# Cross-attention of a decoder block: row maxima of two heads in one reduction, two banks for transposed scores, shifted projections, one-hop rows of maxima

## The chip, the cores and the metric

The kernel runs on one core of a Trainium2 chip. The metric is the time of one execution on the device in microseconds (us), as a median of runs; lower is better.

## What is computed

A decoder layer on x of shape (8, 256, 512): x + self-attention(norm(x)), then x + cross-attention(norm(x), ctx), then x + gated feed-forward(norm(x)) with weights put through an NF4 quantization. The change is mostly in the cross-attention, which treats a batch's (256, 512) matrix as 256 channels by 512 positions:

```python
q = jnp.einsum('oc,bct->bot', Wq, target) + bq[None, :, None]      # 16 heads of 16 channels
k = jnp.einsum('oc,bcs->bos', Wk, source) + bk[None, :, None]
v = jnp.einsum('oc,bcs->bos', Wv, source) + bv[None, :, None]
dot = jnp.einsum('bhdt,bhds->bhts', q, k) / math.sqrt(HEAD_DIM)
mask = target_mask[:, :, :, None] * source_mask[:, :, None, :]
dot = mask * dot - (1.0 - mask) * NEG
amap = jax.nn.softmax(dot, axis=-1) * mask
out = jnp.einsum('bhts,bhds->bhdt', amap, v)
```

So there are 8 batches x 16 heads of 512 x 512 scores.

## The kernel before, in words

The program has three stages behind one another: `self_attention` (until about 1460 us), `cross_attention` (1304 to 1757) and `feed_forward`. Engines run their own instruction lists and wait on semaphores; each list is written out by hand.

In the cross-attention, Q and K of a batch lie in SBUF as stacks: of each head 16 high, 16 high and 16 low rows, then rows for biases and masks, two heads in the two halves of the partitions (even heads at 0, odd ones at 64), so that matmuls of an even and an odd head run beside one another. Row 53 of the Q stack holds the negated maximum of each score row. Four heads form a quad (`u` or `t`; QUADS = 32, four per batch), and a quad has four steps `q`, one for each 128 rows. In what follows t is the quad under way, b its batch (t // 4), and G = 4 * (t % 4) + q the step in its batch, 0 to 15.

For each quad u = t + 2 (LEAD = 2) direct scores are computed (`row_scores`, L1699 to L1706) into `pm`, three PSUM banks, one matmul and one bank per head, and VectorE reduces each bank to a row maximum (`row_max`, L1608 to L1614). When all 16 are there, TensorE turns them (`turn_max`, L1708 to L1711), VectorE negates them into `mT` (`max_rows`, L1616 to L1620), and SP sends them to DRAM, waits for that, and sends them from there to row 53 of Q (`rows`, L1402 to L1410). For the quad t itself the scores are computed again, transposed and with the maxima in them (`dot`, L1713 to L1720), into `pd`, three PSUM banks; ScalarE makes the exponentials (`exponent`, L1469 to L1472) into eight slots of `E`; and TensorE multiplies by the values and a column of ones (`weighted`, L1722 to L1735) into `pa`, one step behind. ScalarE copies `pa` to `raw` after each quad (`take_weighted`, L1474 to L1478), SP spreads that to `att` and `sums` (`spread`, L1412 to L1418), VectorE inverts the sums in four parts (`invert`, L1622 to L1626), and POOL multiplies, divides and adds to x (`divide_and_add`, L1520 to L1532).

TensorE's list for a step is: two transposed scores, (at q = 0 the turn of the maxima), two direct scores, the other two transposed scores, the other two direct scores, then perhaps a projection, then the weighted sums of the step before:

```python
after(pe, exp_done, n - 2)
mm(pd[:, n % 3, :], K[b % 3][z, hp, q * P:(q + 1) * P], Q[b % 3][z, hp, :], ...)      # dot
after(pe, pm_done, k - 2)
mm(pm[:, k % 3, :], Q[b % 3][z, hp, q * P:(q + 1) * P], K[b % 3][z, hp, :], ...)      # row_scores
```

Batch b + 2 is prepared meanwhile. Of its six projections (Q, Q, K, K, V, V, one bank `pp`) TensorE does one in each of the steps G = 5 to 10 (`project`, L1681 to L1697). VectorE takes the statistics of x at G = 0 and 1, normalises at 3 and 4 and takes the projections at 5 to 10 (L1563 to L1606). ScalarE makes high parts at 6 to 9 (`high`), POOL low parts (`low`) and the values (`values`) in the order of L1548 to L1558. SP fills the stack in twelve pieces of 256 KB at the steps of `FILLS` and `LATE` (L1369, L1370), loads the context at G = 3 and the x and mask of batch b + 3 at G = 13, and sends the sums of the last quad at q = 0 and the maxima at q = 1 (L1434 to L1456). Before the loop the stage loads its constants (seven transfers, all of which TensorE waits for ahead of the first value projection, L1744), computes the maxima of quads 0 and 1, and projects batch 1.

At the end of the self-attention POOL makes the low part of the last output (`low_out`, L657 to L660) from a second copy by ScalarE (L556). The feed-forward loads two identity matrices of its own (L1814, L1869), and TensorE waits for the first ahead of its first transposition (L2012).

## Time and profile before

| | |
|---|---|
| median of 3 runs | 2346.96 us (2342.14 to 2351.12) |
| the profiled execution | 2347.5 us, its span 2345.7 us |
| TensorE busy / mean granted clock | 2167.7 us (92%) / 0.959 |
| VectorE busy | 1597.0 us (68%) |
| ScalarE busy | 797.7 us (34%) |
| GpSimd (POOL) busy | 761.3 us (32%) |
| maxima, 512 reductions | 316.5 us of VectorE |
| exponentials, 512 | 264.8 us of ScalarE as far as recorded |

A busy engine may be waiting inside overlapping instructions, and matmuls overlap, so shares of the span say little; what counts is which wait ends last in each stage. PE is TensorE, PEld its weight loads, DVE VectorE, ACT ScalarE, POOL GpSimd and SP the engine that issues most transfers. In a timeline the columns are start in us, duration in us, engine, line and operation, written tile and read tiles, count of merged instructions, and in brackets the idle time before and what ended it.

### The profile page before, as it was taken

Reading aid. Unit: us, or ns where it says so; the run is one execution under the profiler, and the core shown is the slowest. Engines: PE = TensorE matmul, PEld = TensorE weight load, DVE = VectorE, ACT = ScalarE, POOL = GpSimd, SP = SyncE. Lnnn points to the kernel's source line nnn. Section 1 sums busy time; section 2 is a strip of 40 time slices with the busy share of each in tenths; the row PEclk is TensorE's granted clock in tenths of the full one; section 3 lists DMA queues with packets and bytes.
Section 4 is the critical chain, followed back from the end, with each engine's and each line's share of the span. In section 5 each row is a group of like instructions: output and inputs, shape, how many; then the busy total and the mean of one; then the engine's idle time right before and its main releaser. Section 6 shows DMA issues by size and latency. Waiting matters only on the chain. (4 is left out here: it accounts for less than half of the span.)

```text
span 2345.7 us, 35412 instructions
## 1 busy us (share of the span) xinstructions
PE 2167.7 (92%) x11638; PEld 1524.1 (65%) x11638; DVE 1597.0 (68%) x2871; ACT 797.7 (34%) x1845; POOL 761.3 (32%) x533
## 2 busy tenths in 40 slices
PE   6899999999999999999999997599888899879998
PEld 4677777778787777778778785233333333267776
DVE  6658888788786558788788774477777778542221
ACT  1323323322323323323323322155555546642221
POOL 3235334434444334434434433211122221212121
PEclk9999999999999999999999998798989978989999
DMA  5211011011102201011101006634555434311110
GB/s 197 87 40 52 16 49 51 24 40 51 46 19 99 82 20 52 24 41 51 43 22 51 32 4 118 114 64 81 93 107 90 87 74 84 99 60 54 54 36 19
DMA packets 58981, 142.27 MB, mean 61 GB/s; under 512 B 9118, under 2 KB 23910, under 8 KB 53894
## 3 DMA queue, kind: packets, MB, share of 16 engines
q1 hardware_dynamic: 57142, 138.98, 23.4%
q10 hardware_dynamic: 1744, 2.08, 0.3%
q8 instruction: 52, 0.85, 0.2%
q14 instruction: 43, 0.35, 0.1%
HBM read 89.93 MB, written 17.55 MB: 46 GB/s over the span
## 5 line engine op out<-in xcount | busy, mean ns | idle before, releaser
L1614 DVE TENSOR_REDUCE x_mx<-x_pm 128x1 f32<-128x512 f32 x512 | 316.5, 680 | 58.2 <-PE x_pm L1706 55.8
L1472 ACT ACTIVATE x_E<-x_pd 128x512 f32<-128x512 f32 x512 | 264.8, 604 | 214.1 <-PE x_pd L1720 213.4
L1083 PE MATMUL a_pj<-q_big,a_wqk_h 128*128 128x512 f32 x1024 | 290.1, 405 | 1.4 <-POOL a_wqk_l L628 1.4
L1099 PE MATMUL a_pj<-a_wvg_h,q_big 128*128 128x512 f32 x1024 | 286.0, 406 | 1.1 <-DVE a_rm L787 1.0
L1099 PEld LDWEIGHTS a_pj<-a_wvg_h,q_big 128*128 128x128 f32 x1024 | 185.4, 188 | 51.8 <-DVE a_rm L787 2.4
L787 DVE TENSOR_TENSOR a_rm<-a_pj,a_rope 128x1024 f32<-128x1024 f32 x128 | 155.7, 1218 | 79.9 <-PE a_pj L1083 78.5
L1083 PEld LDWEIGHTS a_pj<-q_big,a_wqk_h 128*128 128x128 f32 x1024 | 182.9, 188 | 40.8 <-POOL a_wqk_l L628 1.9
L520 ACT ACTIVATE a_v<-a_pj 128x256 f32<-128x256 f32 x128 | 49.1, 384 | 415.6 <-PE a_pj L1099 415.6
L660 POOL TENSOR_TENSOR a_ogl<-a_ogf,a_ogh 128x512 fp32r<-128x512 f32 x64 | 81.7, 1298 | 285.4 <-ACT a_ogf L556 285.4
L1734 PE MATMUL x_pa<-x_E,x_vx 128*32 128x512 f32 x1024 | 152.2, 670 | 0.0
L859 DVE TENSOR_TENSOR a_acc<-a_po,a_acc 128x512 f32<-128x512 f32 x128 | 85.9, 687 | 92.7 <-PE a_po L1212 92.7
L1099 PE MATMUL a_pj<-a_wvg_l,q_big 128*128 128x512 f32 x512 | 140.3, 396 | 0.0
L1083 PE MATMUL a_pj<-q_big,a_wqk_l 128*128 128x512 f32 x512 | 140.1, 395 | 0.0
L1706 PE MATMUL x_pm<-x_K,x_Q 53*128 53x512 f32 x320 | 112.9, 484 | 20.8 <-DVE x_mx L1614 19.3
L1720 PEld LDWEIGHTS x_pd<-x_Q,x_K 54*128 54x128 f32 x320 | 46.7, 197 | 125.9 <-ACT x_E L1472 71.9
L1720 PE MATMUL x_pd<-x_Q,x_K 54*128 54x512 f32 x320 | 110.5, 503 | 17.0 <-ACT x_E L1472 17.0
L793 DVE RECIPROCAL a_enz<-a_mid 128x512 f32<-128x512 f32 x32 | 107.2, 3351 | 16.8 <-PE a_mid L1067 16.8
L1852 POOL TENSOR_TENSOR f_hl<-f_hf,f_hh 128x512 fp32r<-128x512 f32 x44 | 56.7, 1288 | 189.0 <-ACT f_hh L1899 189.0
L547 ACT ACTIVATE a_sq<-a_po 128x128 bf16<-128x128 f32 x256 | 67.2, 277 | 134.9 <-PE a_po L1124 133.9
L1099 PEld LDWEIGHTS a_pj<-a_wvg_l,q_big 128*128 128x128 f32 x512 | 96.4, 188 | 23.4
L1083 PEld LDWEIGHTS a_pj<-q_big,a_wqk_l 128*128 128x128 f32 x512 | 96.0, 187 | 23.4
L1974 DVE TENSOR_TENSOR f_hf<-f_pb,f_sil 128x512 f32<-128x512 f32 x44 | 30.4, 691 | 117.3 <-PE f_pb L2063 117.3
(219 smaller groups left out, 4624.9 us busy)
## 6 DMA issues: line engine op xcount, KB each, us to landing
a_qk_raw<-in_wqk SPq DMA_DIRECT2D x16, 1024.0 KB, 5.5
a_vg_raw<-in_wvg SPq DMA_DIRECT2D x16, 1024.0 KB, 4.9
a_wo_raw<-in_wo SPq DMA_DIRECT2D x16, 512.0 KB, 3.7
x_Q<-x_hi SPq DMA_DIRECT2D x20, 256.0 KB
x_K<-x_hi SPq DMA_DIRECT2D x20, 256.0 KB
a_acc<-in_w SPq DMA_DIRECT2D x6, 704.0 KB, 4.4
a_wt<-in_w SPq DMA_DIRECT2D x24, 176.0 KB, 2.3
weights_scratch<-a_wt SPq DMA_DIRECT2D x24, 176.0 KB, 1.9
```

The lines of the kernel that those rows point to most:

```text
L547: nc.scalar.activation(sq[:, 4 * b + i, :], po[:, b, i * P:(i + 1) * P], ACT.Square, accum_out=ms[:, 4 * b + i:4 * b + i + 1]).then_inc(sq ...
L660: nc.gpsimd.tensor_tensor(ogl[:, h, :], ogf[:, h, :], ogh[:, h, :].bitcast(F32), ALU.subtract).then_inc(ogl_done, 1)
L787: nc.vector.tensor_tensor(turned, pb, table, ALU.mult).then_inc(roped_m, 1)
L793: nc.vector.reciprocal(enz[:, p], ps[:, 0, :].rearrange("p (t m) -> p t m", t=4)).then_inc(enz_done, 1)
L859: nc.vector.tensor_tensor(a, po[:, tt % 2, :], a, ALU.add).then_inc(added, 1)
L1083: last = mm(pj[:, j % 2, :], wa[:, c, j * P:(j + 1) * P], xa[:, c, p * UT:(p + 1) * UT], start=k == 0, stop=k == 11)
L1099: last = mm(pj[:, tt % 2, :], xa[:, c, t0:t0 + P], wa[:, c, :], start=k == 0, stop=k == 11)
L1472: nc.scalar.activation(E[:, n % ESLOTS, :], pd[:, n % 3, :], ACT.Exp, scale=XD ** -0.5).then_inc(exp_done, 1)
L1614: nc.vector.reduce_max(mx[:, u % 2, at:at + 1], pm[:, k % 3, :], AX_X).then_inc(pm_done, 1)
L1706: mm(pm[:, k % 3, :], Q[b % 3][z, hp, q * P:(q + 1) * P], K[b % 3][z, hp, :], start=True, stop=True).then_inc(pm_ready, 1)
L1720: mm(pd[:, n % 3, :], K[b % 3][z, hp, q * P:(q + 1) * P], Q[b % 3][z, hp, :], start=True, stop=True).then_inc(dot_ready, 1)
L1734: last = mm(pa[32 * i:32 * i + 32, 0, :], vx[:, b % 3, q, head(t, i)].rearrange("p d k -> p (d k)"), E[:, k % ESLOTS, :], start=q == 0, st ...
```

## The change

- `pm` gets four banks, used as two pairs. The direct scores of two heads go to the two banks of a pair, and one reduction takes the maxima of both (256 reductions of 1024 elements instead of 512 of 512). TensorE waits for VectorE once per pair, for the pair before the last. Slots are counted as 9 per quad instead of 17.
- `pd` gets two banks instead of three: a transposed score waits for the exponential two before it instead of three.
- The rows of maxima go from `mT` to Q directly; the DRAM scratch is gone. VectorE writes `mT` only when the last copy has landed.
- Batch b + 2: projections at G = 7 to 12 in the order K, K, Q, Q, V, V; statistics at G = 5 and 6; both normalisations at G = 8; high parts at 8 to 11; POOL's second divide between the low parts of K and Q; fills at 10 to 15 and one piece at 0; x of batch b + 2 loaded at G = 2. Reciprocals at G = 7 to 12, in the last two batches at 2 to 5 and 10 to 13. x is stored at G = 3 and 15.
- The identities and the value weights are loaded once, in the self-attention, into tiles that all stages share; TensorE's wait for the constants moves from before the first value projection to before the first projection of batch 1.
- At the end of the self-attention VectorE makes the last low part, out of PSUM, ahead of its normalisation, and ScalarE's second copy is dropped there.

The diff, cut to its core:

```diff
+            act.dma_start(wv_t[:], wv).then_inc(kept_in, 16)
+            act.dma_start(identb[:], identb_in).then_inc(kept_in, 16)
...
+            def low_last(l):
+                for h in range(2):
+                    dve.wait_ge(ogh_done, 2 * l + h + 1)
+                    nc.vector.tensor_tensor(ogl[:, h, :], po[:, h, :], ogh[:, h, :].bitcast(F32), ALU.subtract).then_inc(ogl_done, 1)
...
                 gated(m, pm)
+                low_last(m)
                 normalised(5)
...
-        pd, pm, pa, pp = banks("pd", 3), banks("pm", 3), banks("pa"), banks("pp")
+        pd, pm, pa, pp = banks("pd", 2), banks("pm", 4), banks("pa"), banks("pp")
...
+        def maxima_slot(u, q, pair):
+
+            return 9 * u + 2 * q + pair
...
+        def order(b):
+
+            return (2, 3, 0, 1, 4, 5) if b > 1 else (0, 1, 2, 3, 4, 5)
+
         def projected(b, j):
 
-            return 6 * b + j - 4
+            return 6 * b + order(b).index(j) - 4
+
+        def halved(b, w):
+
+            return 4 * (b - 1) + order(b).index(2 * w + 1) + 1
...
+        def inverses(b, G):
+
+            if b + 2 < B:
+                due = {7: (-1, (0, 1)), 8: (-1, (2,)), 9: (-1, (3,)), 10: (0, (0,)), 11: (0, (1, 2)), 12: (0, (3,))}
+            else:
+                due = {**{2 + i: (-1, (i,)) for i in range(4)}, **{10 + i: (0, (i,)) for i in range(4)}}
+            n, parts = due.get(G, (0, ()))
+            return 2 * b + n, (parts if 2 * b + n >= 0 else ())
 
         block = s.enter_context(nc.Block())
 
-        FILLS = {8: ((0, 0),), 10: ((0, 1), (0, 2)), 11: ((0, 3), (0, 4)), 14: ((0, 5), (1, 0)), 15: ((1, 1), (1, 4))}
-        LATE = {0: ((1, 5),), 2: ((1, 2), (1, 3))}
+        FILLS = {10: ((1, 0), (1, 1)), 11: ((1, 4), (1, 5)), 12: ((0, 0), (0, 1)), 13: ((0, 2),), 14: ((0, 3), (1, 2)), 15: ((1, 3), (0, 4))}
+        LATE = {0: ((0, 5),)}
...
-                sp.dma_start(max_dram[u % 2], mT[:].bitcast(F32)).then_inc(max_out, 16)
-                sp.wait_ge(max_out, 16 * u + 16)
                 for e in range(2):
                     sp.dma_start(Q[b % 3][64 * e + 53:64 * e + 54, 2 * g:2 * g + 2].rearrange("p h t -> p (h t)").bitcast(F32),
-                                 max_dram[u % 2, 8 * e:8 * e + 8, :].rearrange("(o a) t -> o (a t)", o=1)).then_inc(row_in[u % 2], 16)
+                                 mT[8 * e:8 * e + 8].bitcast(F32)).then_inc(row_in[u % 2], 16)
...
-                    if q == 3 and t >= 4 and t % 2 == 0:
-                        store(t // 2 - 2)
+                    if b and G in (3, 15):
+                        store(2 * b - 2 + (G == 15))
                     if b and b + 1 < B:
                         stack(b + 1, LATE.get(G, ()))
                     if b + 2 < B:
+                        if G == 2 and b:
+                            load_x(b + 2)
                         if G == 3:
                             load_c(b + 2)
                         if G in (6, 7):
                             mask_rows(b + 2, G - 6)
                         stack(b + 2, FILLS.get(G, ()))
-                        if G == 13 and b + 3 < B:
-                            load_x(b + 3)
...
-                    if 6 <= G < 10 and t // 4 + 2 < B:
-                        high(t // 4 + 2, G - 6)
+                    if 8 <= G < 12 and t // 4 + 2 < B:
+                        high(t // 4 + 2, order(2)[G - 8])
...
+                    low(b + 2, 2)
+                    low(b + 2, 3)
+                if b:
+                    divide_and_add(2 * b - 1)
+                if b + 2 < B:
+                    low(b + 2, 0)
+                    low(b + 2, 1)
                     values(b + 2, 0)
                     values(b + 2, 1)
-                if b:
-                    divide_and_add(2 * b - 1)
...
             def row_max(u, q):
-                for i in range(4):
-                    k, at = maxima_slot(u, q, i), 8 * (i % 2) + 4 * (i // 2) + q
+                for pair in range(2):
+                    k, at = maxima_slot(u, q, pair), 4 * pair + q
                     dve.wait_ge(pm_ready, k + 1)
-                    if u >= 2 and q == 0 and i == 0:
+                    if u >= 2 and q == 0 and pair == 0:
                         dve.wait_ge(pm_ready, turned_slot(u - 2) + 1)
-                    nc.vector.reduce_max(mx[:, u % 2, at:at + 1], pm[:, k % 3, :], AX_X).then_inc(pm_done, 1)
+                    two = 2 * (k % 2)
+                    nc.vector.reduce_max(mx[:, u % 2, at:at + 9:8], pm[:, two:two + 2, :], AX_X).then_inc(pm_done, 1)
 
             def max_rows(u):
                 k = turned_slot(u)
                 dve.wait_ge(pm_ready, k + 1)
-                after(dve, max_out, 16 * u)
-                nc.vector.tensor_scalar(mT[:], pm[0:16, k % 3, 0:P], -1.0, None, ALU.mult).then_inc(pm_done, 1)
+                if u:
+                    dve.wait_ge(row_in[(u - 1) % 2], 32 * ((u - 1) // 2 + 1))
+                nc.vector.tensor_scalar(mT[:], pm[0:16, 2 * (k % 2), 0:P], -1.0, None, ALU.mult).then_inc(pm_done, 1)
...
-                    if q >= 2 and t >= 2 and t % 2 == 0:
-                        invert(t // 2 - 1, q - 2)
-                    if q < 2 and t >= 3 and t % 2 == 1:
-                        invert((t - 3) // 2, q + 2)
                     G = 4 * (t % 4) + q
+                    n, parts = inverses(b, G)
+                    for i in parts:
+                        invert(n, i)
                     if b + 2 < B:
-                        if G < 2:
-                            norm_stats(b + 2, G)
-                        if 3 <= G < 5:
-                            norm(b + 2, G - 3)
-                        if 5 <= G < 11:
-                            take_projection(b + 2, G - 5)
+                        if 5 <= G < 7:
+                            norm_stats(b + 2, G - 5)
+                        if G == 8:
+                            norm(b + 2, 0)
+                            norm(b + 2, 1)
+                        if 7 <= G < 13:
+                            take_projection(b + 2, order(2)[G - 7])
...
-                after(pe, pm_done, k - 2)
+                if i % 2 == 0:
+                    after(pe, pm_done, k - 1)
                 e, hp = h % 2, h // 2
                 z = slice(64 * e, 64 * e + STACK_K - 1)
-                mm(pm[:, k % 3, :], Q[b % 3][z, hp, q * P:(q + 1) * P], K[b % 3][z, hp, :], start=True, stop=True).then_inc(pm_ready, 1)
+                last = mm(pm[:, 2 * (k % 2) + i % 2, :], Q[b % 3][z, hp, q * P:(q + 1) * P], K[b % 3][z, hp, :], start=True, stop=True)
+                if i % 2:
+                    last.then_inc(pm_ready, 1)
 
             def turn_max(u):
                 k = turned_slot(u)
-                pe.wait_ge(pm_done, max(k - 2, maxima_slot(u, 3, 3) + 1))
-                nc.tensor.transpose(pm[:, k % 3, 0:P], mx[:, u % 2, :], ident[:]).then_inc(pm_ready, 1)
+                pe.wait_ge(pm_done, max(k - 1, maxima_slot(u, 3, 1) + 1))
+                nc.tensor.transpose(pm[:, 2 * (k % 2), 0:P], mx[:, u % 2, :], ident[:]).then_inc(pm_ready, 1)
...
-                after(pe, exp_done, n - 2)
+                after(pe, exp_done, n - 1)
                 e, hp = h % 2, h // 2
                 z = slice(64 * e, 64 * e + STACK_K)
-                mm(pd[:, n % 3, :], K[b % 3][z, hp, q * P:(q + 1) * P], Q[b % 3][z, hp, :], start=True, stop=True).then_inc(dot_ready, 1)
+                mm(pd[:, n % 2, :], K[b % 3][z, hp, q * P:(q + 1) * P], Q[b % 3][z, hp, :], start=True, stop=True).then_inc(dot_ready, 1)
...
             quad_scores(0, 1)
-            pe.wait_ge(const_in, N_CONST)
             project(0, 4)
             quad_scores(0, 2)
             project(0, 5)
             quad_scores(0, 3)
+            pe.wait_ge(const_in, N_CONST)
...
-                    if 5 <= G < 11 and b + 2 < B:
-                        project(b + 2, G - 5)
+                    if 7 <= G < 13 and b + 2 < B:
+                        project(b + 2, order(2)[G - 7])
```

## Rows read from the trace of the kernel before

**Rows 1.** Page, costliest groups (the last columns: busy us, mean ns of one; idle time before).

```profile
L1614 DVE TENSOR_REDUCE x_mx<-x_pm 128x1 f32<-128x512 f32 x512 | 316.5, 680 | 58.2 <-PE x_pm L1706 55.8
...
L1472 ACT ACTIVATE x_E<-x_pd 128x512 f32<-128x512 f32 x512 | 264.8, 604 | 214.1 <-PE x_pd L1720 213.4
...
L787 DVE TENSOR_TENSOR a_rm<-a_pj,a_rope 128x1024 f32<-128x1024 f32 x128 | 155.7, 1218 | 79.9 <-PE a_pj L1083 78.5
```

**Rows 2.** Stretches: length, busy PE, PEld, DVE, ACT, POOL, clock, DMA share, GB/s.

```profile
1788.00:1801.00 13.00, 11.89 (x70) 4.44 (x70) 11.89 (x20) 8.97 (x18) 3.83 (x3) 1.00 0.81 152
...
1584.60:1946.00 361.40, 321.22 (x1470) 122.73 (x1466) 269.52 (x452) 186.90 (x362) 79.02 (x75) 0.89 0.49 88
```

**Rows 3.** Timeline of ScalarE, copies after quads 0, 3, 23 and 31.

```profile
1538.99 0.60 ACT L1478 ACTIVATE x_raw<-x_pa 128x512 f32<-128x512 f32 x1 [0.92 <-PE x_pa L1734]
...
1588.11 0.60 ACT L1478 ACTIVATE x_raw<-x_pa 128x512 f32<-128x512 f32 x1 [0.92 <-PE x_pa L1734]
...
1949.63 0.60 ACT L1478 ACTIVATE x_raw<-x_pa 128x512 f32<-128x512 f32 x1 [2.09 <-PE x_pa L1734]
...
2047.39 0.60 ACT L1478 ACTIVATE x_raw<-x_pa 128x512 f32<-128x512 f32 x1 [1.14 <-PE x_pa L1734]
```

**Rows 4.** Timeline of TensorE and ScalarE, an undisturbed step without a projection.

```profile
1791.14 0.50 PE L1720 MATMUL x_pd<-q_big 54*128 54x512 f32 x2
...
1791.48 0.39 PE L1706 MATMUL x_pm<-x_K,x_Q 53*128 53x512 f32 x2
...
1791.67 2.07 ACT L1472 ACTIVATE x_E<-x_pd 128x512 f32<-128x512 f32 x4 [1.05 <-PE x_pd L1720]
...
1792.33 0.50 PE L1720 MATMUL x_pd<-q_big 54*128 54x512 f32 x1 [0.23 <-ACT x_E L1472]
...
1793.33 1.06 PE L1734 MATMUL x_pa<-x_E,x_vx 128*32 128x512 f32 x8
...
1794.33 0.49 PE L1720 MATMUL x_pd<-q_big 54*128 54x512 f32 x2
```

**Rows 5.** Timeline of TensorE, a step without direct scores (quad 30).

```profile
2030.51 0.73 PE L1720 MATMUL x_pd<-x_Q,x_K 54*128 54x512 f32 x3
2031.69 0.50 PE L1720 MATMUL x_pd<-x_Q,x_K 54*128 54x512 f32 x1 [0.45 <-ACT x_E L1472]
2032.12 1.07 PE L1734 MATMUL x_pa<-x_E,x_vx 128*32 128x512 f32 x8
```

**Rows 6.** Timeline of TensorE, a step with a projection (the next one starts at 1761.20).

```profile
1756.36 0.50 PE L1720 MATMUL x_pd<-q_big 54*128 54x512 f32 x2
...
1758.29 1.98 PE L1690 MATMUL x_pp<-q_xs,x_wq 128*128 128x512 f32 x4
```

**Rows 7.** Timeline of VectorE and TensorE, steps G = 2 to 5 of batch 3.

```profile
1739.76 0.95 DVE L1626 RECIPROCAL x_sums<-x_sums 128x128 f32<-128x128 f32 x1 [2.60 <-DMA x_sums<-x_raw]
...
1743.53 0.79 PE L1720 MATMUL x_pd<-q_big 54*128 54x512 f32 x2
...
1748.82 0.79 PE L1720 MATMUL x_pd<-q_big 54*128 54x512 f32 x2
```

**Rows 8.** Timeline of VectorE, first quad.

```profile
1523.52 0.69 DVE L1571 BATCH_NORM_STATS2 x_stats<-x_xt 128x6 f32<-128x512 f32 x1 [19.60 <-DMA x_mb<-in_mask]
```

**Rows 9.** Groups by line, 1500 to 2030 us (columns as in rows 1).

```profile
L1600 DVE SCALAR_TENSOR_TENSOR x_lo<-x_pp,x_bqk,x_mb 128x512 f32<-128x512 f32 x24 | 18.0, 749 | 21.2 <-PE x_pp L1690 21.2
```

**Rows 10.** Stretch of SP's view: length, clock, DMA share, GB/s.

```profile
1500.00:1504.00 4.00, 1.00 1.06 122
```

**Rows 11.** Timeline of POOL, end of the self-attention.

```profile
1448.20 2.48 POOL L660 TENSOR_TENSOR a_ogl<-a_ogf,a_ogh 128x512 fp32r<-128x512 f32 x2 [3.53 <-ACT a_ogf L556]
```

**Rows 12.** Timeline of SP and TensorE, start of the feed-forward.

```profile
2058.74 0.34 SPq L1814 DMA_DIRECT2D f_identb<-in_identb  x1
...
2060.41 0.61 PE L2030 MATMUL f_pa<-f_identb,w_raw 128*128 128x128 bf16 x4 [13.06 <-DMA f_identb<-in_identb]
```

**Rows 13.** Timeline of TensorE, start of the cross-attention.

```profile
1469.65 3.78 PE L1695 MATMUL x_pp<-x_wv,q_xs 128*128 128x256 f32 x8 [3.05 <-DMA x_bqk<-in_bqk]
```

74 lines of the change are left out of this document (31 added, 43 removed).

## The prediction

> **What bounds the kernel now.** I read the page, then stretches, then the raw copies, then single steps. On the page the maxima are the largest group of VectorE (512 x 680 ns) and the exponentials the largest of ScalarE (604 ns each) [rows 1]. The stretches show that in the middle of cross-attention (361.4 of the 586 us from 1462 to 2048) VectorE is busy for 269.5 us, ScalarE for 186.9 and TensorE's mean granted clock is only 0.89, whereas 13 undisturbed us have clock 1.00 and VectorE busy for 11.89 [rows 2]: no engine fills the middle, so waits do. The raw copies mark the ends of quads: 361.5 us for batches 1 to 5 (quads 4 to 23), so 72.3 us per batch, where a plain beat (below) makes 12.8 us a quad [rows 3]. I call one step (t, q) a beat: 16 in a batch, 6 with a projection.
>
> An undisturbed plain beat lasts 3.19 us (1791.14 to 1794.33) [rows 4]. Its chain, from the first score matmul at T: the first exponential starts at T+0.53 and ends 0.60 later; the fourth transposed score waits for it (three banks), starts at T+1.19; the fourth direct score waits for a bank that VectorE frees and starts about T+1.77; 0.42 later (the step from a last score to the weighted sums, 2031.69 to 2032.12 in [rows 5]) come the weighted sums, 1.00 us; then the next beat. A beat with a projection lasts 4.84 us, 1.92 of them the projection, before which there are 1.93 us (1756.36 to 1758.29) [rows 6]. So a batch without a wait would take 10 x 3.19 + 6 x 4.84 = 60.9 us; 11.4 us are lost per batch.
>
> They are lost so: VectorE stands 2.60 us at a reciprocal for the DMA of the sums, which SP issued behind stacking transfers; the direct scores' banks are not freed, TensorE idles with it, its clock falls to half (the 1.2 GHz level), and the next beats run slow (1743.53 to 1748.82 is 5.3 us, the next one, with a projection, to 1756.36 is 7.5) [rows 6, 7]. In the first quad the same thing happens once, larger: VectorE waits 19.60 us for the x and mask of batch 2, and TensorE behind it [rows 8].
>
> **The change, part by part.**
>
> 1. *Two banks for the transposed scores.* This costs time. Each score now waits for the exponential two before it. The third score waits for the first exponential (T+1.19), the fourth for the second. Four exponentials span 2.07 us, 0.49 apart [rows 4], so the second ends at T+0.53+0.49+0.60 = T+1.62, and the fourth score starts at T+1.68. The last direct score needs the same rows of the array and starts 0.34 later (T+2.02), as pairs do there (1791.14 to 1791.48); weighted sums at T+2.44; next beat at T+3.44. Plain: 3.44 instead of 3.19. With a projection: 2.44+1.92+1.00 = 5.36 instead of 4.84. In the last quads, which have no direct scores, a beat takes 1.61 to its weighted sums (2030.51 to 2032.12) and their 1.00, so 2.61 [rows 5]; now T+1.68+0.42, so 3.10. Bounds: 2.9 and 4.8 if the second exponential were hidden, 3.6 and 5.5 if the second exponential follows a full 0.60 behind the first and the last score 0.42 behind the one before it. I take the worked value: each piece has its row.
>
> 2. *Maxima of two banks at once.* 512 x 0.60 us of spacing become 256 operations. The nearest row is 128x1024 out of two banks, 1218 ns [rows 1]; spacing about 1.14, and 1.36 if it were twice the old duration. VectorE gains 2.41-2.28 = 0.13 us a beat, or loses 0.3. On the path this is worth nothing by itself: what matters is that four banks let the direct scores of a beat start without a maximum of the same beat. VectorE in the fullest beat (G=8): 2.3, a reciprocal 0.95, a projection 0.75 and the short rows of maxima make 4.3, and two normalisations by at most 0.75 each 5.8, over 5.36 by 0.4 in one beat per batch, which the next beat with its 4.0 takes back; G=7 and 11 have 2.3+1.9+0.75 = 4.95 [rows 7, 9]. With 1.36 each is 0.4 longer, G=8 then costs some 0.5 us.
>
> 3. *Reciprocals at G=7 to 12, statistics at G=5, projections at G=7 to 12, load of x at G=2, fills at 10 to 15.* The sums issued at G=0 are now wanted seven beats later, those of G=8 at G=10, before fills begin. Each stacking piece of 256 KB takes 2.1 us at the 122 GB/s of [rows 10]; the fills ask for 2 pieces in a projection beat (4.2 us in 5.36) and for 5 in the plain beats 13 to 15 (10.5 us in 10.3), so the backlog stays at some 2 us. On SP the rows of a quad go out ahead of the fills of that beat; the load of x (768 KB, about 6 us) has three beats. On POOL the second divide now stands between the low parts of K and Q: it needs the reciprocals of G=9 and ends (three passes of some 1.24 us each, as in [rows 11]) in G=10, before the high part of Q (end of G=10). I find no new wait on the path, so batches 1 to 5: 10 x 3.44 + 6 x 5.36 = 66.6 each, 333 against 361.5: **-28.5**.
>
> 4. *Direct maxima rows.* One SBUF to SBUF hop in place of two through DRAM: SP stood for the landing of the first hop, with everything behind it in its queue; now it does not. No row prices a direct hop; between nothing and the whole second hop it is hidden in calm beats, since the copy has three beats (10 us) to land, so I take nothing. It counts only in the first quad (part 5).
>
> 5. *Start of the stage.* The identity and the value weights are loaded earlier (two issues more on ScalarE's queue at the very start of the kernel, while the first x is still under way: nothing, and without that cover under the 1.67 us that separate issue and use in [rows 12]), and TensorE waits for constants only before the first key or query projection. Now it stands 3.05 us and then runs two projections at half clock (3.78 us each instead of 1.98) [rows 6, 13]: 3.05+1.80+1.80 = 6.65, and some 0.4 from the pairs that no longer wait for a bank. So the first rows of maxima go out about 7 us earlier. The stacking and x loads after it are one row of DMA at full share, ending with the mask at 1523.5 [rows 8, 10]; they end at about 1516.5. The rows of quad 1 are queued behind them, so that quad 1 begins at 1517, where it began 3.5 us before its neighbour's raw copy of 1538.99, at about 1535.5 [rows 3]. TensorE will be idle before it (quad 0 has nothing to wait for now and is done by about 1505), so a half clock again: 1.2 us on the first beat. Its raw copy comes at 1517+3.5+1.2 = 1521.7 instead of 1538.99: **-17.3**. Bounds: -10 if the start gains nothing (the transfers then end at 1523.5 as now) and 0 if something else holds quad 0; -24 if the 7 us come twice.
>
> 6. *Rest of batch 0.* Six projections in quads 1 to 3 as before: 6 x 3.44 + 6 x 5.36 = 52.8, plus 2.5 for the half clock, against 49.1: **+6.2**.
>
> 7. *Batches 6 and 7.* Now 97.8 us from 1949.63 to 2047.39. Then: six quads of 4 x 3.44 = 13.76, quad 30 at 12.4, quad 31 8.9 + 1.5: 105.4, so **+7.6**. (Now the first of them also has a stall, which goes.)
>
> 8. *Edges.* The last low part of self-attention leaves POOL (2.48 us for two, until 1450.7) for VectorE out of PSUM (two of 0.69): output projections begin at 1449.4 instead of behind 1450.7, partly at half clock: **-1.0** [rows 11]. In the feed-forward the first turn waits for the identity until 2060.41 although issues began at 2058.74: **-1.6** [rows 12].
>
> Sum: -28.5-17.3+6.2+7.6-1.0-1.6 = -34.6. The profiled execution took 2347.5 us (span 2345.7 and 1.8 outside it), the median of the runs is 2346.96; 2347.5-34.6 = 2312.9, **2313 us**.
>
> **A rule against the change.** TensorE was granted full speed through the plain beats of 1788 to 1801 [rows 2], although each has a wait of 0.23 us for an exponential and another for a maximum [rows 4]; the beats get longer with the same work in them. The Trainium skill, TensorE: Matmul & The Clock Gate, section "A second HAM failure mode: psum-queue depth-cycling", says that a kernel which cycled through PSUM banks with small idle gaps in each iteration kept falling to half clock and back. By that rule the sum loses its sign; by the rows it stands, since the falls here follow waits of 2.60 and 19.60 us [rows 7, 8].
>
> **Rivals.**
> - *Half clock in plain beats* (slower than before). Mechanism: the fourth score's wait thins TensorE's work until the clock stays at half. A slow beat costs the 5.3 us of [rows 7] instead of 3.44, 1.85 more. From 19 such beats on (34.6/1.85) the change is a loss; with 46, half of the plain ones, 2398 us. For it: no beat of 3.44 us exists in the trace. Against: the quads at 2030, which have no direct scores at all, hold matmuls of 0.50 and 0.73 us, as at full clock [rows 5]. Chance 0.10.
> - *The stalls stay in another beat.* The sums or the x land late again, or quad 1 gets nothing from the start. If half of the 11.4 us per batch stays, 28 us come back: about 2342 us. For it: the DMA engines are at a share near 1 while a stack is filled [rows 10]. Chance 0.14.
> - *The second exponential is hidden*, beats stay at 3.19 and 4.84: 92 x 0.25 + 36 x 0.52 = 42 us less, 2271 us. Against: the order of exponentials and banks leaves no room. Chance 0.06.
> - *The change does not do what it says* (quad 1 is held by something I have not seen, so that the start is worth nothing): 2330 us. Chance 0.05.
>
> **Numbers.** The forecast has 0.65, its own range 2298 to 2332. A measurement of this kernel tells 0.5% (11.7 us) from no change: faster means under 2335. Faster: 0.65+0.06+0.05, and 0.01 of the second rival (its small end) = 0.77; same: the rest of that rival, 0.13; slower: the first, 0.10. Range for 8 in 10: 2286 to 2350, which takes in the second rival above, and below the gain of part 5's far end with a part of the third rival.
>
> **What would show it.** Raw copies 13.8 us apart in quads 25 to 29 (now 12.7) and 12.4 in quad 30; the fourth transposed score at T+1.68, ended by an exponential; reductions of about 1.2 us, 256 of them; raw copies of quads 3 and 23 some 333 us apart; no wait of VectorE for sums or the mask; the clock of the middle near 1. I would be wrong if plain beats stayed at 3.2, if batches took 70 us or more, if TensorE idled over 2.5 us inside a batch, or if quad 1 began before 1510 or after 1530.

## The result and the profile after

| | kernel before | kernel after |
|---|---|---|
| median, run side by side on one chip | 2352.26 us (20 runs, 2342.14 to 2371.45) | 2341.53 us (20 runs, 2330.48 to 2353.51) |
| the profiled execution | 2347.5 us | 2345.58 us, its span 2343.8 |
| TensorE's mean granted clock | 0.959 | 0.959 |
| VectorE / ScalarE / POOL busy | 1597.0 / 797.7 / 761.3 us | 1591.3 / 810.0 / 758.0 us |

The ratio is 0.9949, with a 95% interval of [0.9929, 0.9968]: 10.7 us faster by the medians, where the sum had forecast 34.6. The sign is right and the size is not a third of it. Ratios here and below are taken over the executions, less those more than 1.5% above the fastest of their kernel (five of the twelve of one experiment, none elsewhere), and so need not equal the quotient of the medians. The two profiled executions differ by 1.9 us only. How much of that is chance comes out below, since three kernels that share the code of the middle give three lengths for it.

The costliest groups of the page of the kernel after (columns as in [rows 1]):

```profile
L1639 DVE TENSOR_REDUCE x_mx<-x_pm 128x2 f32<-128x1024 f32 x256 | 311.1, 1222 | 102.3 <-PE x_pm L1733 102.0
L1493 ACT ACTIVATE x_E<-x_pd 128x512 f32<-128x512 f32 x512 | 278.2, 596 | 205.7 <-PE x_pd L1749 194.7
```

One reduction of 1024 elements takes 1222 ns, against 680 ns for one of 512 [rows 1], and the group falls from 316.5 to 311.1 us. Back to back, two of the new ones take 2.43 us (from 1588.45) and four of the old ones 2.42 (from 1740.63 in the kernel before), so VectorE gains nothing a step, where part 2 had 0.13 us.

ScalarE's copies after quads 0, 3, 23 and 31, against [rows 3]:

```profile
1523.59 0.60 ACT L1499 ACTIVATE x_raw<-x_pa 128x512 f32<-128x512 f32 x1 [1.65 <-PE x_pa L1763]
...
1576.13 0.60 ACT L1499 ACTIVATE x_raw<-x_pa 128x512 f32<-128x512 f32 x1 [0.66 <-PE x_pa L1763]
...
1933.75 0.60 ACT L1499 ACTIVATE x_raw<-x_pa 128x512 f32<-128x512 f32 x1 [0.66 <-PE x_pa L1763]
...
2047.36 0.60 ACT L1499 ACTIVATE x_raw<-x_pa 128x512 f32<-128x512 f32 x1 [2.76 <-PE x_pa L1763]
```

They give the account of the profiled execution, term by term:

| stretch | before | after | change | forecast |
|---|---|---|---|---|
| to the first copy | 1538.99 | 1523.59 | -15.4 | -17.3 and the -1.0 of self-attention's end |
| quads 1 to 3 | 49.1 | 52.5 | +3.4 | +6.2 |
| batches 1 to 5 | 361.5 | 357.6 | -3.9 | -28.5 |
| batches 6 and 7 | 97.8 | 113.6 | +15.8 | +7.6 |
| from the last copy to the end | 298.3 | 296.4 | -1.9 | -1.6 |

Two terms failed, the third and the fourth, and by 24.6 and 8.2 us they make up the whole shortfall.

Stretches of the kernel after: the middle as in [rows 2], then two stretches inside (same columns):

```profile
1584.60:1946.00 361.40, 327.50 (x1478) 115.70 (x1476) 268.74 (x296) 196.38 (x364) 78.45 (x75) 0.91 0.51 90
1589.50:1610.00 20.50, 19.72 (x61) 5.82 (x60) 12.83 (x17) 7.63 (x15) 0.71 (x1) 0.50 0.15 35
2016.00:2046.00 30.00, 25.89 (x85) 7.09 (x89) 3.39 (x4) 14.82 (x27) 3.81 (x3) 0.50 0.25 75
```

The clock of the middle is 0.91 (0.89 before), where the prediction wanted it near 1. There are still stretches at 0.50, the 1.2 GHz level: one of them begins in the first steps of batch 1's second quad, another fills the last two quads, where the kernel before had none.

Timeline of the kernel after, G = 3 and 4 of batch 1 (TensorE, ScalarE, VectorE), with SP's issues of stacking pieces and of the row of maxima:

```profile
1567.37 1.33 SPq L130 DMA_DIRECT2D x_Q<-x_hi  x2
1568.74 1.61 SPq L130 DMA_DIRECT2D x_K<-x_lo  x2
1570.40 0.60 SPq L130 DMA_DIRECT2D x_Q<-x_lo  x1
...
1578.00 0.60 SPq L130 DMA_DIRECT2D x_Q<-x_lo  x1
...
1578.70 1.44 SPq L1430 DMA_DIRECT2D x_Q<-x_mT  x2
...
1582.74 0.50 PE L1749 MATMUL x_pd<-x_Q,x_K 54*128 54x512 f32 x2
1583.08 0.39 PE L1733 MATMUL x_pm<-x_K,x_Q 53*128 53x512 f32 x2
...
1583.27 2.27 ACT L1493 ACTIVATE x_E<-x_pd 128x512 f32<-128x512 f32 x4 [1.05 <-PE x_pd L1749]
...
1583.92 0.98 PE L1749 MATMUL x_pd<-x_Q,x_K 54*128 54x512 f32 x2 [0.46 <-ACT x_E L1493]
1584.41 0.72 PE L1733 MATMUL x_pm<-x_K,x_Q 53*128 53x512 f32 x2
1585.06 1.07 PE L1763 MATMUL x_pa<-x_E,x_vx 128*32 128x512 f32 x8
...
1587.21 0.50 PE L1749 MATMUL x_pd<-x_Q,x_K 54*128 54x512 f32 x2 [1.08 <-DMA x_Q<-x_mT]
```

Read the step from 1582.74: the third score starts 1.18 later, as worked out (T+1.19), and the fourth follows it within the same group of 0.98 us, behind the second exponential (its weights are loaded at T+1.67, forecast T+1.68); the weighted sums are at T+2.32 (forecast T+2.44). Its neighbour of the same kind, from 1579.41 to 1582.74, lasts 3.33 (forecast 3.44). This part of the prediction was right to 0.1 us. The step itself then ends 4.47 after it began, with TensorE idle for 1.08 us. What it waits for is the row of maxima of quad 5, which SP issued at 1578.70, behind a stacking piece at 1578.00 and five others issued from 1567.37 to 1571.00. The row holds 8 KB (4 heads x 512 numbers); it is there 8.5 us after its issue, and TensorE had come to the wait after 7.4.

That is the queue and not the direct hop. The copy of the sums issued at 1577.35, two issues ahead of the row, landed after 8.0 us; at G = 0 of batches 1 to 5 this copy takes 8.0, 7.9, 6.9, 7.1 and 8.4 us, at the start of the other quads there 2.7 to 3.1. The two longest waits for a row (below) are in the batches with 8.0 and 8.4. With nothing of the stack ahead of it, a row issued at 2005.14 (quad 31 in the experiment with four banks) was used at 2008.55, 3.4 us later.

Here is what follows the wait. The steps of the quad, from 1587.21 on, last 4.20, 4.98, 4.98 and 8.69, three of them at 0.50 of the clock; an undisturbed quad there takes 15.3 us and this one 22.8. Of five batches, three have it (quads 5, 17 and 21: 22.8, 21.3 and 22.0 us), all three behind a wait for the row of 1.08, 0.58 and 1.14 us at the end of G = 3. In the other two the wait is 0.38 and 0.40 us and the clock stays. Quad 21 begins so:

```profile
1869.62 0.80 PE L1749 MATMUL x_pd<-x_Q,x_K 54*128 54x512 f32 x2 [1.14 <-DMA x_Q<-x_mT]
```

The stalls had moved: from VectorE at G = 2 and 3, which stood for the sums [rows 7], to TensorE at the end of G = 3, which stands for the maxima of the quad that begins at G = 4.

### The profile page after: what moved, and what is told of

It reads as the page before. It is cut to its first block and busy times, and to the rows that moved or that the text cites. A ratio compares the mean times of both kernels' runs of the same rounds, so it can differ in the third digit from the quotient of the medians.

```text
span 2343.8 us, 35117 instructions
## 1 busy us (share of the span) xinstructions
PE 2182.0 (93%) x11638; PEld 1512.6 (65%) x11638; DVE 1591.3 (68%) x2617; ACT 810.0 (35%) x1843; POOL 758.0 (32%) x531
## 5 line engine op out<-in xcount | busy, mean ns | idle before, releaser
L1639 DVE TENSOR_REDUCE x_mx<-x_pm 128x2 f32<-128x1024 f32 x256 | 311.1, 1222 | 102.3 <-PE x_pm L1733 102.0
L1493 ACT ACTIVATE x_E<-x_pd 128x512 f32<-128x512 f32 x512 | 278.2, 596 | 205.7 <-PE x_pd L1749 194.7
L520 ACT ACTIVATE a_v<-a_pj 128x256 f32<-128x256 f32 x128 | 49.1, 384 | 416.1 <-PE a_pj L1107 416.1
L1749 PE MATMUL x_pd<-x_Q,x_K 54*128 54x512 f32 x320 | 128.0, 555 | 34.6 <-ACT x_E L1493 31.3
L1107 PEld LDWEIGHTS a_pj<-a_wvg_l,q_big 128*128 128x128 f32 x512 | 96.7, 189 | 23.4
L1091 PEld LDWEIGHTS a_pj<-q_big,a_wqk_l 128*128 128x128 f32 x512 | 96.0, 187 | 23.4
L1220 PE MATMUL a_po<-a_wo_h,a_ogh 128*128 128x512 f32 x256 | 106.3, 415 | 1.5 <-DVE a_ogl L860 1.5
```

What stands on the lines that cost most here:

```text
L1091: last = mm(pj[:, j % 2, :], wa[:, c, j * P:(j + 1) * P], xa[:, c, p * UT:(p + 1) * UT], start=k == 0, stop=k == 11)
L1107: last = mm(pj[:, tt % 2, :], xa[:, c, t0:t0 + P], wa[:, c, :], start=k == 0, stop=k == 11)
L1220: last = mm(po[:, tt % 2, :], oa[:, h, tt * P:(tt + 1) * P], wa[:, h, :], start=k == 0, stop=k == 5)
L1493: nc.scalar.activation(E[:, n % ESLOTS, :], pd[:, n % 2, :], ACT.Exp, scale=XD ** -0.5).then_inc(exp_done, 1)
L1639: nc.vector.reduce_max(mx[:, u % 2, at:at + 9:8], pm[:, two:two + 2, :], AX_X).then_inc(pm_done, 1)
L1749: mm(pd[:, n % 2, :], K[b % 3][z, hp, q * P:(q + 1) * P], Q[b % 3][z, hp, :], start=True, stop=True).then_inc(dot_ready, 1)
```

## The experiments

The theory: SP's queue is what holds the middle, because the stacking pieces of G = 15 and 0 stand ahead of the row that SP sends at G = 1, and the half clock is a consequence of that wait. The rival: the two banks thin TensorE's work so that its clock falls by itself, wait or no wait (the prediction's first rival), and the row's wait is a bystander. The first group of runs separates these. Every median below has its kernel before on the same chip beside it. The number in the heading is the time saved against that.

### Two stacking pieces behind the row (34.7 us)

```diff
-        FILLS = {..., 14: ((0, 3), (1, 2)), 15: ((1, 3), (0, 4))}
-        LATE = {0: ((0, 5),)}
+        FILLS = {..., 14: ((0, 3), (1, 2)), 15: ((1, 3),)}
+        LATE = {1: ((0, 4), (0, 5))}
```

> Edit: in the changed kernel the two last low pieces of the Q stack leave SP in step G = 1 behind the row of maxima, instead of at G = 15 and 0 ahead of it. Theory A (the row of maxima for the quad that begins at G = 4 lands late behind stacking pieces; TensorE waits 0.4 to 1.2 us there and its clock falls to half for some 14 to 20 us): step G = 3 takes 3.3 to 3.5 us in every batch instead of 3.8 to 4.5, quads 5, 17 and 21 take 15.3 us instead of 21 to 23, and the run is 15 to 25 us faster than the changed kernel (about 2320 us). Rival B (steps with two score banks are too thin and lose the clock by themselves): the wait goes, but half-clock stretches of the same total length stay in the middle and the time stays within 5 us of the changed kernel.

Measured: 2318.91 us (6 runs, 2309.67 to 2325.17) against 2353.65, ratio 0.9842 [0.9803, 0.9881]. Its stretch of batches 1 to 5:

```profile
1584.00:1900.00 316.00, 286.52 (x1390) 102.88 (x1388) 252.49 (x280) 183.03 (x340) 73.57 (x70) 0.99 0.53 96
```

The step at G = 3 is 3.3 us in every batch, and quads 5, 17 and 21 take 15.3 like their neighbours. The batches last 65.8, 67.4, 65.7, 67.3 and 65.7 us, 331.9 together, against 333 forecast. The sums copied at G = 0 land after 4.9 to 6.5 us now, instead of 6.9 to 8.4. The same matmuls in the same 3.33 us steps hold the clock at 0.99 once the row is in time. So it was the wait for the row, half a microsecond to one, that brought it down, and not the two banks by themselves. This is the run that decides the matter for the middle. Moving two entries of a table makes the kernel 34.7 us faster than before. That this is also what the sum had promised (34.6) is chance: in the profiled execution the middle gives 29.7 us (forecast 28.5), while batches 6 and 7 still cost 14.1 us instead of 7.6.

### Work added in the last two quads (16.6 us)

In batches 6 and 7 nothing is stacked, but quads 30 and 31 ran at half clock. They have no direct scores any more, so TensorE has only four scores and eight narrow matmuls a step. Timeline of TensorE in the kernel after, quad 31 (against [rows 5]):

```profile
2027.54 0.79 PE L1749 MATMUL x_pd<-x_Q,x_K 54*128 54x512 f32 x2
...
2029.02 1.28 PE L1749 MATMUL x_pd<-x_Q,x_K 54*128 54x512 f32 x2 [0.69 <-ACT x_E L1493]
...
2030.23 1.93 PE L1763 MATMUL x_pa<-x_E,x_vx 128*32 128x512 f32 x8
...
2032.09 0.79 PE L1749 MATMUL x_pd<-x_Q,x_K 54*128 54x512 f32 x2
```

A step takes 4.55 us here, 0.69 of it idle behind an exponential; at full clock it was forecast at 3.10, and the first step of quad 30, still at full clock, takes 3.10. The experiment adds four direct scores per step, whose result nobody reads:

```diff
+                        else:
+                            for k in range(2):
+                                h = head(t, i + k)
+                                z = slice(64 * k, 64 * k + STACK_K - 1)
+                                mm(pm[:, k, :], Q[b % 3][z, h // 2, q * P:(q + 1) * P], K[b % 3][z, h // 2, :], start=True, stop=True)
```

> Edit: the changed kernel with four direct-score matmuls more in each step of the last two quads, where there are none: their results go to two free banks and nobody reads them. Theory A (without direct scores a step of 3.1 us has too little work for the full clock): with the useless matmuls the clock stays at full, a step takes 3.3 us instead of 4.55, quads 30 and 31 take 27 to 28 us together instead of 36, the run is some 8 us faster than the changed kernel. Rival D (the clock falls there for another reason, or the steps are slow for lack of exponentials): the two quads stay at 36 us or become longer by the added work, 1 us a step, 44 us.

Measured: 2337.07 us (10 runs, 2326.28 to 2343.22) against 2353.65, ratio 0.9921 [0.9891, 0.995]. Timeline of TensorE in its quad 30 (L1799 are the added matmuls):

```profile
2009.32 0.50 PE L1749 MATMUL x_pd<-x_Q,x_K 54*128 54x512 f32 x2
...
2010.51 0.98 PE L1749 MATMUL x_pd<-x_Q,x_K 54*128 54x512 f32 x2 [0.45 <-ACT x_E L1493]
2011.00 0.73 PE L1799 MATMUL x_pm<-x_K,x_Q 53*128 53x512 f32 x2
...
2012.65 0.50 PE L1749 MATMUL x_pd<-x_Q,x_K 54*128 54x512 f32 x2
```

The added matmuls fill gaps; the step is 3.33 us at full clock. Quads 30 and 31 take 27.8 us instead of 36.1, with twice as many score matmuls. By the ratios (0.9921 and 0.9949) the kernel is some 6.6 us faster than after, which two intervals that overlap don't prove. The trace fits the theory that thin work lets the clock fall, but it is one execution, and another experiment (two banks alone, below) holds the full clock with the same thin steps and nothing added. So it isn't shown that thin work alone is the cause, only that the fall comes there and needs no wait for a transfer. To that extent the prediction's first rival had a point.

### Four banks for the scores of the last two quads (34 us)

The maxima's banks are free there, so the four transposed scores of a step go to four banks:

```diff
+        def score_bank(n):
+
+            if n < LASTQ or n % 4 < 2:
+                return pd[:, n % 2, :]
+            return pm[:, n % 4 - 2, :]
...
-                after(pe, exp_done, n - 1)
+                after(pe, exp_done, n - 3 if n >= LASTQ + 4 else min(n - 1, LASTQ))
```

> Edit: the changed kernel; in the last two quads, where the direct scores need no banks, the transposed scores go round in four banks (their two and two of the direct ones). Theory A: a step is bound by the exponentials (4 x 0.49 plus what is left of the chain) and takes 2.2 to 2.6 us at full clock, the two quads 18 to 22 us instead of 36, the run 12 to 16 us faster than the changed kernel. Rival D (the clock falls there whatever the banks): steps of 3.5 us or more with the granted clock at half, at most 6 us gained.

Measured: 2319.55 us (4 runs, 2315.07 to 2321.31) against 2353.65, ratio 0.9849 [0.9802, 0.9896]. Timeline of TensorE in quad 30:

```profile
2002.19 0.50 PE L1757 MATMUL x_pd<-x_Q,x_K 54*128 54x512 f32 x2
...
2004.21 0.50 PE L1757 MATMUL x_pd<-x_Q,x_K 54*128 54x512 f32 x2
...
2006.59 0.50 PE L1757 MATMUL x_pd<-x_Q,x_K 54*128 54x512 f32 x2
```

Steps of 2.0 to 2.4 us at full clock: the copies from quad 27's to quad 31's stand 42.1 us apart, against 59.6 in the kernel after, which is 17.5 us. The same matmuls in less time kept the clock here. All four runs of this kernel are faster than every run of the kernel after (2321.31 at most against 2330.48 at least), by 22 us in the medians where 12 to 16 were expected.

This run and the one above give the spread of the middle as well. Up to quad 29 their code is that of the kernel after. Batches 1 to 5 took 347.0 us in this profiled execution, 345.3 in the one above and 357.6 in the kernel after: the first wait for the row brought down the clock in all three, the later ones in two batches of the kernel after, in one here and in none above. So the profiled execution of after has a long middle; the other two gain 15 and 16 us there, not 3.9. It also lies above its median (2345.58 against 2341.53), and that of the kernel before below its own (2347.5 against 2352.26), which is why medians differ by 10.7 us and the profiled executions by 1.9.

### Two banks alone, in the kernel before (43 us slower)

```diff
-        pd, pm, pa, pp = banks("pd", 3), banks("pm", 3), banks("pa"), banks("pp")
+        pd, pm, pa, pp = banks("pd", 2), banks("pm", 3), banks("pa"), banks("pp")
...
-                after(pe, exp_done, n - 2)
+                after(pe, exp_done, n - 1)
```

> Edit: the kernel before with two banks instead of three for the transposed scores, nothing else. Theory A (the second wait for an exponential is a cost by itself): undisturbed plain steps 3.3 us instead of 2.94 to 3.20 (3.12 on average), projection steps 5.25 instead of 4.85, the last quads 3.1 a step instead of 2.6 or, with the clock at half, 4.55; in all 30 to 45 us slower than the kernel before (about 2385 us). Rival E (the steps of the kernel before are held by VectorE and by late transfers, so that the third bank hides nothing): within 8 us of the kernel before.

Measured: 2396.24 us (4 runs, 2374.86 to 2408.56) against 2353.46, ratio 1.0198 [1.0151, 1.0245]. The profiled execution was the fastest of the four and is 27 us above the profiled one of before. Timeline of TensorE, a plain step of quad 29 (from 2040.91) and one without direct scores of quad 31 (from 2060.03):

```profile
2040.91 0.50 PE L1720 MATMUL x_pd<-x_Q,x_K 54*128 54x512 f32 x2
...
2044.24 0.50 PE L1720 MATMUL x_pd<-x_Q,x_K 54*128 54x512 f32 x2
...
2060.03 0.49 PE L1720 MATMUL x_pd<-x_Q,x_K 54*128 54x512 f32 x2
2061.21 0.99 PE L1720 MATMUL x_pd<-x_Q,x_K 54*128 54x512 f32 x2 [0.68 <-ACT x_E L1472]
2062.13 1.06 PE L1734 MATMUL x_pa<-x_E,x_vx 128*32 128x512 f32 x8
2063.13 0.50 PE L1720 MATMUL x_pd<-x_Q,x_K 54*128 54x512 f32 x2
```

Undisturbed plain steps are 3.33 to 3.43 here too, against 2.94 to 3.39 with three banks: the third bank is worth 0.2 us in a plain step. With a projection a step takes 5.25 here against 4.85, but two of the six in a batch of the kernel before take 5.3 already (1766.05 to 1771.36), so it is worth 0.4 us in four of six.

These last quads also show that the fall of the clock isn't certain. The steps without direct scores take 3.10 us, as forecast, and all of them run at full clock (1.00 from 2047.5 to 2073.5). With the same two banks and the same thin steps the clock fell in the kernel after, in the first experiment and in the one on ScalarE's order, after one, two and three such steps. It doesn't take two banks either: with three, steps of 2.61 us held in the kernel before and in the two fastest variants, and in two others (the banks back at three, and the reciprocals' steps alone) quad 31 fell to half clock. With four banks it held in both variants that have them. No run here says what decides it.

### The banks back at three, maxima one head at a time (23 us)

The kernel after, but with three banks for the scores and three single ones for the maxima, so that everything else of the change stands alone:

```diff
-        pd, pm, pa, pp = banks("pd", 2), banks("pm", 4), banks("pa"), banks("pp")
+        pd, pm, pa, pp = banks("pd", 3), banks("pm", 3), banks("pa"), banks("pp")
...
-                nc.vector.reduce_max(mx[:, u % 2, at:at + 9:8], pm[:, two:two + 2, :], AX_X).then_inc(pm_done, 1)
+                nc.vector.reduce_max(mx[:, u % 2, at:at + 1], pm[:, k % 3, :], AX_X).then_inc(pm_done, 1)
...
-                after(pe, exp_done, n - 1)
+                after(pe, exp_done, n - 2)
```

> Edit: the changed kernel with three banks for transposed scores and three single banks for direct ones, one reduction per head, as before; everything else (order of the projections, reciprocals, loads, one-hop rows, start) stays changed. Theory A (the second wait for an exponential costs 0.14 us in a plain step and 0.4 in one with a projection, and buys nothing once the late transfers are moved): plain steps average 3.18 us, projection steps 4.85, quads 24 to 31 take about 98 us instead of 119, and the run is 30 to 40 us faster than the changed kernel (about 2305 us). Rival C (the two-bank maxima are what frees TensorE from VectorE; with single banks VectorE's reciprocals and normalisations at G = 7 to 12 hold the direct scores again): projection steps grow to 5.5 us or more, and the run is not faster than the changed kernel.

Measured: 2330.38 us (12 runs, 2302.41 to 2352.95) against 2353.65, ratio 0.9854 [0.9815, 0.9893]; the ratio counts seven of the twelve, whose median is 2323.05. Faster than after, by 11 to 18 us instead of the expected 30 to 40, and with a spread of 50 us. Its stretch of batches 1 to 5, one of its waits in the timeline, and all of this kind in the list of waits (1575 to 1930 us; total, times, longest):

```profile
1584.00:1930.00 346.00, 320.27 (x1451) 122.36 (x1453) 267.60 (x449) 184.65 (x357) 78.58 (x75) 0.87 0.52 92
```

```profile
1577.38 0.51 PE L1745 MATMUL x_pd<-x_Q,x_K 54*128 54x512 f32 x2 [1.26 <-DMA x_Q<-x_mT]
```

```profile
PE x_pd L1745 <- DMA x_Q<-x_mT: 5.1, 4, 1.3
PE x_pd L1745 <- DMA q_big<-x_mT: 2.5, 2, 1.3
```

The shortest undisturbed steps are back at 2.94 and 4.85, but the row of maxima is then wanted sooner than the same queue can bring it: TensorE waits for it six times, 7.6 us in all, each time at the end of G = 15, where the kernel after doesn't wait, and the mean clock is 0.87. Each of the six waits (1.23 to 1.30 us) was followed by a stretch at half clock, of 3.4 to 37.5 us, and that is where the spread comes from as far as one trace shows. Faster steps alone turned into longer waits.

### The reciprocals' steps alone, in the kernel before (10 us)

```diff
-                    if q >= 2 and t >= 2 and t % 2 == 0:
-                        invert(t // 2 - 1, q - 2)
-                    if q < 2 and t >= 3 and t % 2 == 1:
-                        invert((t - 3) // 2, q + 2)
+                    n, parts = inverses(b, G)
+                    for i in parts:
+                        invert(n, i)
```

with the table of `inverses` from the change, and x stored at G = 3 and 12.

> Edit: the kernel before with the reciprocals in the steps of the changed kernel (G = 7 to 12, in the last two batches 2 to 5 and 10 to 13), and for that the stores of x at G = 3 and 12; banks, projections, fills and the two-hop rows stay. Theory A (moving the reciprocals frees the direct scores at G = 2 and 3, but the row of maxima, two hops behind the stacking pieces, is late next): the waits of 2.6 to 5 us for the sums are gone, and in their place the first transposed score at G = 4 waits 3 to 6 us for the maxima from DRAM, with the half clock behind it; quads 4 to 23 take 345 to 360 us instead of 361.5 and the run gains 0 to 15 us. Rival I (the wait for the sums was the only one): quads 4 to 23 take 305 to 315 us and the run is 45 us or more faster than the kernel before.

Measured: 2339.07 us (7 runs, 2335.5 to 2347.83) against 2349.4, ratio 0.9935 [0.991, 0.9961]. VectorE's wait for the sums in the middle is gone, and at once the next one comes forward. Timeline of TensorE at a G = 4:

```profile
1671.70 0.79 PE L1728 MATMUL x_pd<-x_Q,x_K 54*128 54x512 f32 x2 [3.52 <-DMA x_Q<-maxima_scratch]
```

Batches 1 to 5 take 345.5 us (69.1, 68.5, 71.2, 68.2, 68.5), 16 less than before, with such a wait in each (1.3 to 3.6 us). In the kernel before, TensorE comes to the row later and stands for it in the open only once (1.19 us at 1944.94, shown further down). This one small part brings as much as the whole change did by the medians. Its profiled execution (2347.83) shows none of it, since batches 6 and 7 took 110.7 us instead of 97.8, with quads 24 and 31 at half clock.

### ScalarE's order at G = 8 (37 us)

With the row in time, one long step remained: G = 9, 5.86 us where others with a projection take 5.25. In two batches of the first experiment and three of the kernel after, the clock falls to half for 3.4 us in it, and it takes 7.49. (The expectation below counts these 7.5 us to G = 10; it is the same step.) Timeline of the kernel after there (ScalarE and TensorE), in such a batch:

```profile
1681.42 0.50 PE L1749 MATMUL x_pd<-x_Q,x_K 54*128 54x512 f32 x2
1681.56 0.60 ACT L1499 ACTIVATE x_raw<-x_pa 128x512 f32<-128x512 f32 x1 [2.58 <-PE x_pa L1763]
1682.05 0.62 ACT L1488 ACTIVATE x_hi<-x_lo 128x512 fp32r<-128x512 f32 x1
1682.57 2.26 ACT L1493 ACTIVATE x_E<-x_pd 128x512 f32<-128x512 f32 x4
...
1683.21 0.98 PE L1749 MATMUL x_pd<-x_Q,x_K 54*128 54x512 f32 x2 [1.06 <-ACT x_E L1493]
```

ScalarE makes the copy and then the high part before the exponentials of G = 9, so they start 1.15 after the scores instead of 0.53. On top of the late pieces the experiment puts the high part ahead of the copy, for which ScalarE has to wait anyway:

```diff
-                    if q == 0 and t:
-                        take_weighted(t - 1)
                     if 8 <= G < 12 and t // 4 + 2 < B:
                         high(t // 4 + 2, order(2)[G - 8])
+                    if q == 0 and t:
+                        take_weighted(t - 1)
```

> Edit: the changed kernel with the two late pieces behind the row of maxima (as in the first experiment) and, on ScalarE at G = 8, the high part ahead of the copy of the weighted sums instead of behind it. Theory F (step G = 9 takes 5.86 us since ScalarE begins its exponentials 0.6 us late, and the wait tips the clock to half for one more step of 7.5 us at G = 10 in some batches): G = 9 takes 5.25 us, G = 10 never 7.5, the middle of the run is 1.2 us a batch faster on average, 5 to 10 us in all against the first experiment. Rival G (VectorE, with two normalisations at G = 8, holds G = 9): G = 9 stays at 5.8 us or more.

Measured: 2316.2 us (4 runs, 2304.08 to 2319.41) against 2353.46, ratio 0.9831 [0.9785, 0.9877]. G = 9 takes 5.34, all five batches take 65.2 to 65.3 us, and the clock never falls between 1523 and 1987 us. The medians (2318.9 and 2316.2) can't tell this kernel from the one without the new order; the 5.7 us that it saves over five batches are in the trace alone.

### All three mends together (55 us)

Late pieces, four banks in the tail, ScalarE's order, and VectorE's work at G = 7 to 9 more evenly spread (one normalisation each at 7 and 8, reciprocals one, one, two):

```diff
-                due = {7: (-1, (0, 1)), 8: (-1, (2,)), 9: (-1, (3,)), 10: (0, (0,)), 11: (0, (1, 2)), 12: (0, (3,))}
+                due = {7: (-1, (0,)), 8: (-1, (1,)), 9: (-1, (2, 3)), 10: (0, (0,)), 11: (0, (1, 2)), 12: (0, (3,))}
...
-                        if G == 8:
-                            norm(b + 2, 0)
-                            norm(b + 2, 1)
+                        if 7 <= G < 9:
+                            norm(b + 2, G - 7)
```

> Edit: the changed kernel with the late pieces behind the row of maxima, four banks for the transposed scores of the last two quads, the high part ahead of the copy, and the two normalisations in steps G = 7 and 8. Theory A: the losses add up and go together: middle batches 65.2 us each, the last two quads 18 to 20 us, no half clock between 1540 us and the end of the stage; the run takes about 2295 us, 15 to 25 less than each of the first and fourth experiments alone. Rival B: half-clock stretches of 10 us or more turn up elsewhere and the run stays at 2315 us.

Measured: 2298.51 us (6 runs, 2296.44 to 2303.82) against 2353.46, ratio 0.9767 [0.9735, 0.9798], as expected to 3.5 us. The runs are within 7.4 us of one another, where those of the kernel after spread over 23; in the profiled one the clock doesn't fall from 1534 us to the end of the stage. Batches take 65.2 us each, and the copies of quads 27 and 31 are 42.1 apart.

### The same without the two-bank maxima (79 us)

Now the two-bank part is taken out of that kernel (three banks for the scores, maxima one head at a time), and the pieces are spread so that fewer of them stand before each row:

```diff
-        FILLS = {10: ((1, 0), (1, 1)), 11: ((1, 4), (1, 5)), 12: ((0, 0), (0, 1)), 13: ((0, 2),), 14: ((0, 3), (1, 2)), 15: ((1, 3), (0, 4))}
-        LATE = {0: ((0, 5),)}
+        FILLS = {10: ((1, 0), (1, 1)), 11: ((1, 4), (1, 5)), 12: ((0, 0),), 13: ((0, 1),), 14: ((0, 2), (0, 3)), 15: ((1, 2),)}
+        LATE = {1: ((1, 3), (0, 4)), 3: ((0, 5),)}
```

> Edit: the variant with three banks each and one reduction per head, with the twelve stacking pieces spread so that at most one is ahead of a row of maxima (two at G = 10 and 11, one at 12, 13, 15, two at 14, two at 1 and one at 3), the high part ahead of the copy, and the normalisations in G = 7 and 8. Theory A (its steps of 2.94 and 4.86 us are undone only by 1.3 us waits for rows of maxima at G = 15 and 3, and the half clock after them): middle batches of 59 to 62 us, the run at 2280 to 2295 us, the fastest of all. Rival H (with steps this short the transfers, 25 us of pieces in a batch beside 13 of others, cannot keep up): waits of 1 us or more stay at G = 15 or move to G = 5 and 7, batches of 65 us or more, the run at 2310 us or more.

Measured: 2274.25 us (6 runs, 2271.39 to 2277.39) against 2353.46, ratio 0.9664 [0.9634, 0.9695]. Its stretch of batches 1 to 5, and a plain step of TensorE:

```profile
1576.00:1880.00 304.00, 281.45 (x1458) 111.06 (x1456) 266.68 (x450) 184.80 (x360) 78.69 (x75) 1.00 0.58 105
```

```profile
1688.12 0.50 PE L1744 MATMUL x_pd<-x_Q,x_K 54*128 54x512 f32 x2
...
1689.30 0.50 PE L1744 MATMUL x_pd<-x_Q,x_K 54*128 54x512 f32 x1 [0.21 <-ACT x_E L1493]
...
1690.07 1.06 PE L1758 MATMUL x_pa<-x_E,x_vx 128*32 128x512 f32 x8
1691.06 0.50 PE L1744 MATMUL x_pd<-x_Q,x_K 54*128 54x512 f32 x2
```

2.94 us a step, full clock throughout, batches of 60.9 to 61.0. That is the 60.9 that the prediction worked out for a batch of the kernel before without a wait, but by luck: it is made of ten plain steps of 3.03 us and six of 5.11 on average here, and was worked out from 3.19 and 4.84. The two kernels differ by 24 us (2298.51 against 2274.25); 21 of them are the five batches (60.9 instead of 65.2), and the last two quads, where only the slower kernel has four banks, speak for that one (42.1 against 43.8 from quad 27's copy to quad 31's). So the two-bank maxima, with the bank that they take from the scores, cost time here, and their companions, put in the right places, are worth 79 us. With 512 single reductions VectorE is busy for 266.68 of 304 us, and TensorE waits for its maxima 25 times, never longer than 0.4 us and 7.8 us in all.

### The first quad (82 us)

The remaining long wait is that of quad 1 for its row, behind batch 1's twelve pieces, in the kernel after too:

```profile
1518.47 0.79 PE L1749 MATMUL x_pd<-q_big 54*128 54x512 f32 x2 [12.45 <-DMA q_big<-x_mT]
```

On top of the kernel above, SP now sends eight of the twelve pieces first, and the other four and both loads of x behind the row:

```diff
-            stack(1, WHOLE)
-            load_x(2)
-            load_x(0)
+            stack(1, WHOLE[:8])
...
+                    if t == 0 and q == 1:
+                        load_x(2)
+                        stack(1, WHOLE[8:])
+                        load_x(0)
```

> Edit: the last experiment's fastest variant (three banks each, spread pieces); at the start of the stage SP sends only eight of the twelve pieces of batch 1 ahead of the row of maxima of quad 1, then in the step G = 1 of batch 0 the row, then x of batch 2, the other four pieces and x of batch 0. Theory A (the 16.5 us step at G = 3 of the first quad is the wait for that row behind 5 MB of transfers): the step takes 3 to 5 us, quad 1 begins at about 1507 instead of 1519, and the run is 8 to 15 us faster, about 2262 us. Rival J (the wait only moves: the statistics at G = 5 or the first K projection of batch 2 at G = 7 then stand for the rest of the transfers): 5 us or less are gained, with a wait of 8 us or more in quad 1.

Measured: 2267.16 us (5 runs, 2265.35 to 2267.76) against 2349.4, ratio 0.9635 [0.9608, 0.9662]. Timeline of TensorE, first score of quad 1:

```profile
1509.71 0.50 PE L1746 MATMUL x_pd<-q_big 54*128 54x512 f32 x2 [2.72 <-DMA q_big<-x_mT]
```

The wait is down to 2.72 us, and the first copy of the weighted sums comes 10.4 us sooner than in the kernel above. Behind the wait the clock fell again, so that quad 1 took 23.4 us from copy to copy instead of 18.8, and the end came 5.6 us sooner by the profiled executions (spans 2271.0 and 2265.4), less than the 8 to 15 expected. This is the fastest version of the study: 3.65% less than before.

## Why the prediction was wrong

- **Part 1 (two banks): right.** Plain steps 3.33 to 3.43 against 3.44, with a projection 5.25 against 5.36, and 3.10 without direct scores at full clock. The least disturbed batch of the kernel after (quads 12 to 15) takes 66.2 against 66.6, with steps 0.1 us shorter than worked out and 1.1 us more at G = 3 and G = 9 to make up for it. What was misread is the step with a projection before: 4.84 holds for four of six, the other two take 5.3, so that these steps lose 0.23 us on average and not 0.52. The first exponential and the second stand in the chain as described, and the third rival (the second one is hidden) is out.
- **Part 2 (maxima): right but for a small gain that didn't come.** 1222 ns a reduction, two in 2.43 us where 2.28 were worked out, and nothing on the path by itself.
- **Part 3 (the middle): the step that failed.** It said "On SP the rows of a quad go out ahead of the fills of that beat" and "I find no new wait on the path". The first sentence is true of the fills of the same step and forgets those of the steps before. I had counted 10.5 us of pieces in the 10.3 us of G = 13 to 15 and called some 2 us of backlog harmless, without asking who queues behind it: the row sent at G = 1 has to be there at G = 4, and the pieces of G = 15 and 0 are on the same queue. Part 4 gave the copy "three beats (10 us) to land"; it leaves 2.7 us into G = 1, which left it 7.4, and it took 8.5 from issue to use. Moving two pieces behind it gave 331.9 us for the five batches instead of 357.6, so this oversight is the whole of the shortfall of the term. The 333 of the forecast was then met with two more errors in it that nearly cancel: with G = 9 mended too the batches take 326.1 us, 7 less than forecast, since all steps are 0.1 us shorter, and G = 9 itself, where I hadn't asked in what order ScalarE works, costs 5.7.
- **The half clock as a price.** The second rival was priced as half of the old stalls and called for 2342 us, about the median that came. It is the case that happened, with a chance of 0.14, though with another transfer (it named the sums and x, not the row), and its number fits by luck: it put all 28 us into the middle, where the profiled execution lost 24.6 there and 8.2 at the end. What I had not allowed for was how short a wait the half clock can follow. The prediction's argument against the rule was that the falls here follow waits of 2.60 and 19.60 us [rows 7, 8]. In the kernel after, 0.58 to 1.14 us at the end of a plain step preceded it in three of five batches, and the quad then took 6.0 to 7.5 us more. The trace of the kernel before already had such a case, between two plain steps, with 13.7 us at half clock from 1946.7 on:

```profile
1944.94 0.49 PE L1720 MATMUL x_pd<-q_big 54*128 54x512 f32 x2 [1.19 <-DMA q_big<-maxima_scratch]
```

- **Part 7 (batches 6 and 7): the mis-sized term.** Quads 24 to 27 were right (54.0 against 55.0). Quads 28 to 31 took 59.6 against 50.4: in quads 30 and 31 all steps from the third on took 4.55 us in place of 3.10, at half clock. My argument against the first rival rested on exactly these quads of the kernel before [rows 5], with steps of 2.61 us, full clock. I had lengthened the step by a fifth in part 1 and not asked again. The longer step isn't the whole cause: steps of 3.10 us held the full clock in one variant and steps of 2.61 lost it in two. What was wrong is that one execution at full clock was taken for a proof; the cause stays open. The Trainium skill, TensorE: Matmul & The Clock Gate, section "A second HAM failure mode: psum-queue depth-cycling", says of one kernel that cycled through PSUM banks in each iteration that small idle gaps brought it to half clock again and again. In these quads the rows of the kernel after look like it (0.50 in the stretch 2016 to 2046, and full clock with the gaps filled or with four banks), those of the variant just named don't. For plain steps they don't either: the same 0.46 us wait in each, and clock 0.99 to 1.00 over five batches.
- **Part 5 (start): right.** The first copy came at 1523.59 against 1521.7, quad 1 began at 1518.5 against 1517, and the cause of what stays was named: its row behind the stack of batch 1. TensorE itself came to quad 0 at 1489.35 instead of 1500.2, 10.9 us sooner where part 5 had about 7: one value projection still ran at half clock (3.78), and the pairs that no longer wait for a bank gave more than the 0.4 worked out.
- **Part 6:** +3.4 against +6.2; the steps were 0.1 us shorter than worked out, and of the half clock's 1.95 us (4.98 and 3.63 instead of 3.33 twice) most came before the first copy.
- **Parts 4 and 8.** The direct hop cost nothing that a row shows; by itself it can be over in 3.4 us (above). The feed-forward's first matmul comes at 2058.70 for 2060.41, -1.7 against -1.6. Self-attention's end gave nothing: output projections begin at 1450.45 for 1450.83, and the cross-attention's first matmul at 1462.50 for 1461.89. Timeline of TensorE in the kernel after:

```profile
1450.45 0.76 PE L1220 MATMUL a_po<-a_wo_h,a_ogh 128*128 128x512 f32 x1 [1.50 <-DVE a_ogl L860]
```

VectorE's low part (L860) is now what they wait for, in the place of POOL's.

What stays open: why a wait for the row brings the clock down in one batch and not in another, and what decides the last quads. In the three executions with the code of this middle, no fall followed the six waits of 0.32 to 0.40 us; of the nine of 0.47 to 1.14 us six were followed by one and three were not (0.53, 0.61 and 1.05 us). The stretches differ from run to run of one kernel, and no run here isolates the state of the clock at the moment of the wait.

## What to carry to other kernels

A queue has to be read from the point of view of its smallest urgent transfer: for each one, list what was issued ahead of it in all earlier steps and hasn't landed, not only what shares its own step. When one stall is taken away, ask what was hidden behind it with less slack, because the next wait can return the gain through the clock even if it is much shorter. One profiled execution at full clock doesn't show that the clock is safe there. And where a step has an idle gap per round that nothing fills, one more bank can be worth more than fewer instructions.

## What the runs showed of the hardware

- A wait of TensorE of 0.58 to 1.14 us between two plain steps was followed by 17 to 21 us at the 1.2 GHz level in three batches of five in the kernel after; with the wait gone, the clock was 0.99 over the 316 us of the same steps. Waits of 0.53, 0.61 and 1.05 us in two other executions of the same code were not followed by a fall.
- Steps of four scores and eight narrow matmuls: at 3.10 us each the clock fell to the 1.2 GHz level in three kernels and held 2.4 GHz in a fourth; at 2.61 us it held in three and fell in two; at 2.0 to 2.4 us (four banks) it held in two; and with four more score matmuls in 3.33 us in the one that has them.
- A row of 8 KB from 16 partitions into two was used 8.5 us after its issue behind 256 KB pieces on the same queue, and 3.4 us after it without them.
- VectorE's reduction over two PSUM banks takes 1222 ns. Back to back, two of these take 2.43 us, and four over one bank each 2.42.
